# A graph layer and a mixture-of-experts layer in one kernel: another order for the first three pairs of graphs

## What is computed

```
xn  = layernorm(x)                       # per token
h   = xn @ W.T + b
att = sigmoid(h@a1 [rows] + h@a2 [cols] + att_b) * adj * mask * mask
x   = x + mask * ((att / (att.sum(-1) + 1e-8)) @ h)
xn2 = layernorm(x)
top2, idx = top_k(xn2 @ gate_w + gate_b, 2);  w = softmax(top2)
moe = sum over the 2: w * (relu(xn2 @ w1[e] + b1[e]) @ w2[e] + b2[e])
x   = x + layernorm(xn2 + moe) * gamma + beta
```

## Time and profile before

| | |
|---|---|
| three runs | 456.19, 456.40, 458.34 us; median 456.40 us |
| the profiled execution | 456.47 us, its span (first to last instruction) 454.7 us |
| mean granted TensorE clock | 0.928 |
| busy share of the span | PE 76%, PEld 61%, DVE 65%, ACT 50%, POOL 67% |
| scatters of the front on POOL | 128, busy 123.5 us |

### The profile page before, as it was taken

The page is one execution under the profiler, slowest core; times in us unless marked ns, Lnnn a source line. Parts: engine busy times, 40 slices in busy tenths (PEclk is TensorE's granted clock), DMA queues, the critical chain, the costliest instruction groups (busy, mean ns, idle before and its releaser), DMA issues.

```text
span 454.7 us, 11203 instructions
## 1 busy us (share of the span) xinstructions
PE 343.6 (76%) x2287; PEld 279.0 (61%) x2287; DVE 295.3 (65%) x1466; ACT 228.1 (50%) x704; POOL 303.0 (67%) x331
## 2 busy tenths in 40 slices
PE   4688878877878854200998988988888889888992
PEld 3566767766767753100897777777777778833330
DVE  4687899999999884610476666666555555610664
ACT  3568869978999844100333333333333334311662
POOL 5620767777777777773277777777777777771565
PEclk9999989999999985555799999999999999999998
DMA  7812536645555643496866777777777776316994
GB/s 239 282 59 71 170 137 190 184 162 163 165 174 199 212 151 107 160 234 216 256 184 186 213 218 205 237 211 217 212 222 217 214 232 191 108 37 239 391 347 138
DMA packets 61683, 88.10 MB, mean 194 GB/s; under 512 B 10213, under 2 KB 40859, under 8 KB 61490
## 3 DMA queue, kind: packets, MB, share of 16 engines
q1 hardware_dynamic: 30786, 43.45, 32.5%
q0 software_dynamic: 10720, 25.32, 15.7%
q10 hardware_dynamic: 20112, 18.63, 13.8%
HBM read 55.61 MB, written 32.73 MB: 194 GB/s over the span
## 4 chain that ended last, share of the span: by engine, by line
PE 25%; DVE 20%; issue 13%; DMA 12%; POOL 12%; ACT 5%; ACTq 2%; DVEq 1%; POOLq 1%; SPq 0%
POOL token_y L445 8%; DMA token_y<-yb,xb 5%; PE psum L1265 5%; PE psum L1254 5%; DMA xb<-sorted_x 4%; POOL sorted_x L422 3%; ACT xn L535 3%; PE psum L1167 3%; PE psum L1298 2%; PE psum L1299 2%; DVE i L848 2%; PE psum L1157 2%; DMA out_dram<-xrow 1%; PE psum L1139 1%; DVE newton L812 1%
## 5 line engine op out<-in xcount | busy, mean ns | idle before, releaser
L445 POOL DMA_INDIRECT token_y<-yb,xb x143 | 143.3, 1002 | 58.1 <-issue 35.4
L422 POOL DMA_INDIRECT sorted_x<-xrow,rows x128 | 123.5, 964 | 60.1 <-issue 56.8
L606 ACT ACTIVATE hid<-psum,b_sb 128x256 f32<-128x256 f32 (+1 forms) x188 | 69.2, 419 | 142.7 <-PE psum L1254 72.0
L1265 PE MATMUL psum<-w_sb,hid 128*128 x572 | 83.1, 282 | 7.0 <-ACT hid L606 5.7
L1265 PEld LDWEIGHTS psum<-w_sb,hid 128*128 128x128 f32 x572 | 75.0, 192 | 15.5 <-issue 12.9
L1254 PE MATMUL psum<-xbT,w_sb 128*128 128x256 f32 (+1 forms) x376 | 81.7, 341 | 2.4 <-DVE xbT L1025 2.2
L1034 DVE TENSOR_TENSOR yb<-psum,b_bc 128x256 f32<-128x256 f32 (+1 forms) x94 | 33.9, 360 | 63.0 <-PE psum L1265 59.4
L1254 PEld LDWEIGHTS psum<-xbT,w_sb 128*128 128x128 f32 x376 | 58.2, 194 | 8.3 <-DVE xbT L1025 5.2
L1244 PE MATMUL psum<-ident_aug,xb 128*128 128x128 f32 x143 | 33.5, 292 | 29.6 <-DMA xb<-sorted_x 27.2
L1025 DVE COPY xbT<-psum 128x256 f32<-128x256 f32 (+1 forms) x94 | 33.2, 354 | 23.6 <-PE psum L1244 23.3
L1039 DVE SCALAR_TENSOR_TENSOR yb<-yb,xb 128x128 f32<-128x128 f32 x143 | 46.1, 351 | 3.3
(11 more groups left out here) (168 smaller groups left out, 567.6 us busy)
## 6 DMA issues: line engine op xcount, KB each, us to landing
xb<-sorted_x SPq DMA_DIRECT2D x49, 258.0 KB, 3.1
w_sb<-w_dram ACTq DMA_DIRECT2D x94, 128.0 KB, 2.9
adj_in<-adj_dram SPq DMA_DIRECT2D x32, 256.0 KB
got<-token_y SPq DMA_DIRECT2D x16, 512.0 KB, 5.7
xb<-sorted_x SPq DMA_DIRECT2D x45, 129.0 KB, 2.8
out_dram<-xrow ACTq DMA_DIRECT2D x16, 256.0 KB, 3.4
xmid<-x_dram SPq DMA_DIRECT2D x6, 512.0 KB, 8.0
token_y<-yb,xb POOLq DMA_INDIRECT x143
```

The lines of the kernel that those rows point to most:

```text
L422: pool.indirect_dma_start(sorted_x, bass.IndirectOffsetOnAxis(ap=rows[:, slot, t, k:k + 1], axis=0), xrow[:, slot, k, t, :], None).then_in ...
L445: pool.indirect_dma_start(token_y, bass.IndirectOffsetOnAxis(ap=xb[:, q, t, TO:TO + 1].bitcast(I32), axis=0), yb[:, h, t, :], None, bounds ...
L606: last = act.activation(hid[:, u % RING, c, 0:n], psum[:, 2 + u % 2, c * BT:c * BT + n], ACT.Relu, bias=b1_sb[:, c, e])
L1265: last = mm(psum[:, 4 + u % 2, t * D:(t + 1) * D], hid[:, u % RING, c, t * P:(t + 1) * P], w2_sb[:, e, c * D:(c + 1) * D].rearrange("p a c ...
```

## The change

On PE the first projections of pair 1 and the transposes of pair 2 now come ahead of pair 0's aggregate, the centring of the biases (`centre_b2`) comes after the adjacency of pair 1, and pair 0's second transposes and gate come ahead of pair 1's aggregate, not after it. On DVE `stats_of(3)` comes right after `stats_of(2)`, pair 0's residual and norm come ahead of the bias copy and the gate's set-up, pair 0's routing is taken apart from pair 1's Newton steps and comes earlier, and `stats_of(4)`, `stats_of(5)` and the block `stats_of(6)` with `rstd1_of(5)` each come later, the last two by a turn. On SP the loads of weights 2 and 3 and of adjacencies 1 and 2 are taken out of the loop and put ahead of the wait for the biases. ACT and POOL keep their order.

```diff
@@ SP
             for c in range(EARLY_X + 1, len(XCHUNKS)):
                 load_x(sp, c)
+            for e in range(2, 4):
+                load_w2(e, e % 2)
+                load_adj(e - 1)
             sp.wait_ge(b2_ready, 1)
             sp.dma_start(b2_even, b2_less).then_inc(b2_kept, 16)
-            with sp.Fori(1, PAIRS // 2) as j:
+            with sp.Fori(2, PAIRS // 2) as j:
@@ DVE
             stats_of(1)
             stats_of(2)
+            stats_of(3)
+            attend_all(0)
+            residual(0)
+            norm(variance(0))
             setup_b2()
             setup_gate()
-            stats_of(3)
-            attend_all(0)
+            attend_all(1)
             stats_of(4)
-            residual(0)
-            norm(variance(0))
-            attend_all(1)
-            stats_of(5)
+            choose(one_hot(which(0, largest(0))))
             residual(1)
+            place(0, pick(row_numbers(0)))
             r = variance(1)
             attend_all(2)
-            norm_route_and_place(r, 0)
+            norm(r)
             turn(3)
+            stats_of(5)
+            turn(4)
             stats_of(6)
             rstd1_of(5)
-            for m in range(4, PAIRS + 1):
+            for m in range(5, PAIRS + 1):
                 turn(m)
@@ PE
             project(0, 1, 0)
             transpose_x(1)
-            centre_b2()
-            aggregate(0, 0)
             project(1, 0, 1)
             project_s1(1)
             project(1, 1, 1)
+            transpose_x(2)
+            aggregate(0, 0)
             transpose_adj(1)
-            transpose_x(2)
+            centre_b2()
             project(2, 0, 0)
             project_s1(2)
+            transpose_x2(0, 3)
+            gate(0)
+            project(2, 1, 0)
             aggregate(1, 1)
-            transpose_x2(0, 3)
-            project(2, 1, 0)
+            rank(0)
             transpose_adj(2)
-            gate(0)
             transpose_x(3)
             project(3, 0, 1)
             project_s1(3)
             project(3, 1, 1)
             aggregate(2, 0)
-            rank(0)
             transpose_x(4)
```

## The result

The changed kernel takes 461.15 us (median of 6 runs, 459.70 to 461.75), the kernel before 456.29 us (median of 6 runs beside it, 454.28 to 458.34): ratio 1.0103 with a 95% interval of 1.0072 to 1.0134. It is slower by 1%, some 4.7 us; forecast were 458.8 us and, at most, 461.0; the median lies 0.15 us above that.

The account below looks back on a forecast made before the run. POOL's scatters bound the front, whose end follows the start of a deciding pair (pair 2 before). Moved wait 0.2 plus low clock 2.2 gave 2.4 us on 456.47, 458.9, given as 458.8 us; range 456.2 to 461.0.

Parts of the forecast that it names:

- Pair 0's aggregate, the norm, the pause: On PE and ACT: aggregate ends 0.9 us earlier, second transposes come 2.0 us earlier, and a new PE pause opens before them.
- The clock: On PE after the new pause: lower clock level slows transposes, gate, half projection and pair 1's aggregate, adding 2.2 us.
- The first scatter stays at 45.9 us: On POOL: pair 0's row numbers come some 4 us sooner, its weights do not, so the first scatter does not move.
- 6.72 us that the change does not touch: On ACT: almost gapless work from the copy of pair 3 at 37.88 us to pair 0's weights at 44.60.
- The wait is moved by one pair, not removed: On POOL: later statistics move the wait from before pair 2 to before pair 3, adding 0.2 us.
- 1.3 us to spare: Row numbers on DVE: pair 4 has this margin, and the statistics blocks of pairs 5 to 7 use most of it.
- The sum: Whole kernel: 0.2 us from the moved wait plus 2.2 us from the pause's low clock, 2.4 us slower.
- At nothing: Moved bias copy and gate set-up cost DVE under a microsecond where PE waits anyway; SP's reordered loads cost nothing.
- is passed on unchanged: Behind the last scatter: the stretch to the kernel's end keeps its length.
- The clock did not hold: Rival on PE: the clock holds or returns at once after the pause, leaving only 0.2 us, 456.6 us; chance 19%.
- The wait did not go: Rival on POOL: pair 3's row numbers come by 75.5 us, no wait, front up to 2.4 us earlier, 454.1 us; 9%.
- DVE's statistics did not hold up the scatters: Rival on POOL: scatters stand still through chunk 5's statistics block on DVE, giving about 460.4 us; chance 4%.

Follow-up runs that it names:

- run 1: The changed kernel with five unread matmuls filling TensorE's pause ahead of pair 0's second transposes: 458.2 us, ratio 1.0050 to the kernel before.
- run 8: The changed kernel with pause filled, pair 0's weights early, statistics moved to where DVE idles and last roots a turn later: 454.86 us, ratio 0.9970 to the kernel before.
- run 9: The kernel of run 8 without the unread matmuls in TensorE's pause: 458.2 us, ratio 1.0036 to the kernel before.
- run 5: The changed kernel with the statistics of chunks 5 and 6 put back, pause left unfilled: 459.14 us, ratio 1.0056 to the kernel before.
- run 6: The changed kernel with the statistics of chunks 5 and 6 put back and the pause filled by five unread matmuls: 457.12 us, ratio 1.0025 to the kernel before.
- run 2: The changed kernel with pair 0's weights on ACT taken ahead of the copy of pair 3: 461.14 us, ratio 1.0113 to the kernel before.
- run 3: The kernel before with only the statistics of chunks 5 and 6 moved as in the change: 458.63 us, ratio 1.0056 to the kernel before.
- run 7: The kernel of run 3 with the last roots (pairs 8 and 9) a turn later: 457.26 us, ratio 1.0024 to the kernel before.
- run 10: The kernel of run 8 with pair 0's weights back at their old place behind ACT's copy of pair 4: 455.97 us, ratio 0.9981 to the kernel before.
- run 11: The kernel of run 8 with pair 3's adjacency transposed earlier on PE: 454.96 us, ratio 0.9959 to the kernel before.

## Why the prediction was right or wrong

- **Pair 0's aggregate, the norm, the pause: right.** Forecast: the aggregate over at 23.1 us, second transposes at 30.9, a pause of 4 to 5 us, transposes near 1.1 and gate near 1.9 us at 0.50. Measured: 22.91, 30.74, 4.82, 1.12, 1.86, at 0.50.
- **The clock: mechanism right, its length too short.** I let the level return early in pair 1's aggregate and took 2.2 us between 1.4 and 3.5. It returned only behind it, at about 40.2 us; the aggregate ended at 39.41 us instead of the 35.8 of the upper level, 3.6 us late. Pair 1's row numbers and the first scatter came 3.3 us late by it, not 2.2. By time the pause is worth 2.4 us in run 1, whose profile still has that aggregate at the lower level, 3 in runs 8 and 9, and 1.4 to 2.0 in runs 5 and 6, where chunk 5's block hides a part.
- **"The first scatter stays at 45.9 us": not refuted, but the wrong row.** This was said without the pause, and no run has the changed kernel at the upper level throughout. ACT's copy of pair 3 came at 38.08 us at that level (run 6), close to the 37.9 I worked out. The "6.72 us that the change does not touch" were 6.34 in the changed kernel; run 6 has 7.91 there, by the block that its edit puts before pair 1's residual. So, as far as the runs go, the first scatter is late by the clock. But run 2 shows that the weights could come 4 us sooner for nothing. What counts is the row numbers of pair 1 and after, which the same slow aggregate delays. My sum did carry the delay on to pair 3's row numbers.
- **"The wait is moved by one pair, not removed": right in place, too small in size.** No wait before pair 2, one before pair 3: as forecast, and the turns of 10.3 and 13.2 us were 10.37 and 13.41. Beyond the 3.30 us of pair 1, pair 3 starts on POOL 0.50 us later than before (78.01 to 81.81), where I gave the moved statistics 0.2. A second wait, 0.55 us beyond the fixed gap, stood before pair 7, where I gave nothing. The sentence on the 1.3 us to spare, of which pairs 5 to 7 would "use most", failed: there were 1.15, and they use 1.77. The turns of pairs 5 and 6 carry one block of statistics each (from 89.96 and 100.35 us), that of pair 7 the last roots (111.01 to 113.99 us). Runs 3 and 7 price the moved statistics at 2.6 us by time and put about half of it, with wide intervals, on the roots ahead of pair 7; the traces show 1.05 us of it. Where the rest of the 2.6 lies stays open.
- **The sum.** 0.2 + 2.2 was forecast. In the profile the last scatter is 4.23 us late: 3.30 from the clock, 0.50 and 0.55 from the statistics, less 0.12 from the quicker pace behind pair 3. By time the pause is worth 2.4 to 3 us and the moved statistics 2.1 (run 5 to the change) to 2.6 (run 3), for a loss of 4.7 in all. Both terms were too small, the statistics by far the more.
- **"At nothing".** PE transposes adjacency 1 at 22.75 us without a wait for its load. No run takes back the moves on SP or of the biases alone.
- **What follows the last scatter "is passed on unchanged": nearly.** It took 246.1 us before and 246.7 after, but in the profiles of all kernels between 245.2 and 248.5.
- **The rivals.** The clock did not hold. The wait did not go: pair 3's row numbers came at 80.72 us and not by 75.5. DVE's statistics did not hold up the scatters: DVE's block of statistics from 57.20 us lies under the scatters that start at 57.08, 58.34 and 59.61 us, and they keep the pace of 1.26 and 1.27 us. The rule that I had quoted from the Trainium skill ("SBUF — State Buffer", section "SBUF: two separate sides") is about the time in which VectorE holds the shared port. No row tells whether these statistics hold it, so the pace shows no case of the rule, and it does not speak against it.

## What to carry to other kernels

When a pair's own steps are pulled ahead, look for the row that decides the end, not for the first output: here the first scatter could come 4 us sooner for nothing, and the row numbers of later pairs set the end. A pause that a new order opens on TensorE is part of its price, here 2.4 to 3 us by time. A block of side work should stand where its engine waits in the new order: the change moved statistics out of such a place into turns that had no room, run 6 put a block between a result and the engine that waited for it, and the same order with them in an idle stretch, the pause filled and the weights early beat the kernel before. Where turns are nearly as long as the consumer's pace, add up the spare time turn by turn; three excesses of 0.3 to 1.0 us made a wait three pairs later.

## What the runs showed of the hardware that was not expected

After a pause of 4.82 us TensorE stayed at the lower level from about 30.0 to 40.2 us, through all the work of that stretch, although from 34.0 to 40.0 us PE was busy without a gap. The level also fell without a long pause: behind the gate's matmuls, in the profiles of runs 1, 10 and 11, where the longest pause of PE in the 5 us ahead was 0.77 us. With the same work on PE up to that point it did not fall in runs 6 and 8. Pair 1's aggregate took 3.59, 3.23 and 3.12 us in the first three, 1.95 in the other two.

The Trainium skill ("TensorE: Matmul & The Clock Gate", section "Part 1: The HAM clock gate (the "warmup" mystery)") says of the start of a kernel that the number of its matmuls at the lower level differs from run to run. The executions here agree in that the share of the lower level is not fixed: of the 29 of the kernel before that were taken beside runs 9 to 11, the mean granted clock is between 0.913 and 0.928, with 0.927 in the fastest (454.40 us) and 0.913 in the slowest (459.13 us). One profile is therefore one draw. If the level falls ahead of pair 1's aggregate in some executions of a kernel and not in others, 1.2 to 1.6 us of their spread could come from this aggregate alone; no two profiles of one kernel were taken to show it.
